# Group norm of two recurrent layers: deviations from TensorE, one variance row per head, a narrow inverse

## The reference

```python
xn = ln(x); sx = shifted(xn) - xn                  # token shift
x5 = xn + sx * (maa_stack + low_rank(xn + sx * maa_x))      # five mixes
w = exp(-exp(time_decay + tanh(x5[1] @ dw1) @ dw2))
r, k, v, g = x5[3] @ Wr.T, x5[0] @ Wk.T, x5[2] @ Wv.T, silu(x5[4] @ Wg.T)
att = scan over tokens:  out = r . (u*k*v + s);  s = k*v + w*s
m = mean(att, per head of 8); var = mean((att - m)**2, per head of 8)
att = (att - m) * rsqrt(var + 1e-5) * gn_w + gn_b    # group norm
x = x + (att * g) @ Wo.T
x = x + sigmoid(xr @ Wfr.T) * (relu(xk @ Wfk.T)**2 @ Wfv.T)  # second half
```

## Time and profile before

| what | us |
| --- | --- |
| median of three executions | 3260.69 |
| the three executions | 3263.27, 3260.69, 3254.81 |
| span of the profiled execution, first to last instruction | 3262.3 |
| the one listed execution that is no shorter than this span | 3263.27 |
| PE busy in the span | 2860.0 (88%) |
| DVE busy | 2025.3 (62%) |
| ACT busy | 1415.0 (43%) |
| POOL busy | 657.0 (20%) |

### The profile page before, as it was taken

How to read it: one execution, slowest core, us unless ns; L and a number is a source line. 1 busy time by engine, 2 the same in 40 slices (tenths; PEclk the granted TensorE clock), 3 DMA queues, 4 the chain that set the end, 5 groups by cost and what they waited for, 6 DMA issues and landing times. The chain is left out here.

```text
span 3262.3 us, 63509 instructions
## 1 busy us (share of the span) xinstructions
PE 2860.0 (88%) x18753; PEld 1510.2 (46%) x18753; DVE 2025.3 (62%) x4196; ACT 1415.0 (43%) x3023; POOL 657.0 (20%) x482
## 2 busy tenths in 40 slices
PE   6899999999999999999868888799999997888885
PEld 3344444444444444444334444466666654544443
DVE  4667776776767677677457787344444441168775
ACT  2255555555555555555612221254444443222221
POOL 4221122122112212212023333000000001033331
PEclk8799999999999999999978999799999998899997
DMA  7332433343343333334010000111110100100000
GB/s 211 107 108 75 121 108 94 103 120 102 83 122 108 86 111 111 92 101 102 16 63 1 1 1 1 54 28 34 27 34 27 34 15 29 60 1 6 6 1 12
DMA packets 117234, 205.16 MB, mean 63 GB/s; under 512 B 39765, under 2 KB 84546, under 8 KB 116546
## 3 DMA queue, kind: packets, MB, share of 16 engines
q1 hardware_dynamic: 115010, 198.32, 21.1%
q10 hardware_dynamic: 1920, 2.75, 0.4%
HBM read 156.09 MB, written 44.59 MB: 62 GB/s over the span
## 5 line engine op out<-in xcount | busy, mean ns | idle before, releaser
L596 DVE CUSTOM_DVE_ANT_0 masked<-ps_a,mask 112x750 f32<-112x750 f32 x1024 | 941.8, 936 | 383.4 <-PE ps_a L483 360.0
L556 ACT ACTIVATE probs<-ps_a 128x448 f32<-128x448 f32 (+1 forms) x1536 | 743.2, 542 | 552.7 <-PE ps_a L449 545.4
L483 PE MATMUL ps_a<-ks,q_row 96*112 96x375 bf16 x2048 | 528.3, 341 | 54.1 <-DVE part_max L596 34.9
L449 PE MATMUL ps_a<-q_sc,ks 99*128 99x448 bf16 (+1 forms) x1536 | 451.0, 359 | 52.6 <-ACT probs L556 30.9
L469 PE MATMUL ps_a<-probs,vp 128*32 128x224 f32 x6144 | 381.7, 367 | 1.2 <-ACT probs L556 0.9
L483 PEld LDWEIGHTS ps_a<-ks,q_row 96*112 96x112 bf16 x2048 | 219.9, 132 | 325.4 <-issue 266.6
L2037 DVE CUSTOM_DVE_ANT_0 f_masked<-ps_c,f_mp 112x432 f32<-112x432 f32 x256 | 145.5, 605 | 221.2 <-PE ps_c L1889 218.7
L449 PEld LDWEIGHTS ps_a<-q_sc,ks 99*128 99x128 bf16 (+1 forms) x1536 | 132.3, 100 | 287.1 <-issue 238.4
L236 POOL CAST k_piece<-kv_t 64x1500 bf16<-64x1500 f32 x32 | 45.6, 1426 | 1044.1 <-ACT kv_t L228 1044.1
L469 PEld LDWEIGHTS ps_a<-probs,vp 128*32 128x32 f32 x6144 | 164.6, 111 | 160.3 <-ACT probs L556 60.2
L215 PE MATMUL ps_a<-ctx_t,wkv 128*128 128x375 f32 x512 | 197.3, 511 | 18.6 <-DMA ctx_t<-in_ctx_t 8.5
(11 more groups left out here) (283 smaller groups left out, 3977.6 us busy)
## 6 DMA issues: line engine op xcount, KB each, us to landing
ctx_t<-in_ctx_t SPq DMA_DIRECT2D x32, 1500.0 KB, 8.9
ks<-k_scr SPq DMA_DIRECT2D x64, 562.5 KB, 5.2
mask<-in_mask SPq DMA_DIRECT2D x64, 328.1 KB, 5.5
k_scr<-k_piece SPq DMA_DIRECT2D x64, 281.2 KB, 6.6
k_scr<-k_piece SPq DMA_DIRECT2D x64, 187.5 KB, 6.8
f_context<-in_ctx_t SPq DMA_DIRECT2D x32, 375.0 KB, 3.1
k_scr<-k_piece SPq DMA_DIRECT2D x64, 93.8 KB, 7.1
q_row<-q_scr SPq DMA_DIRECT2D x64, 84.0 KB, 4.4
```

The costliest lines, as they stand in the source:

```text
L449: mm = pe.matmul(out, ks[par][:, j, at], q_sc[par][:, j], start=True, stop=not with_mask)
L483: mm = pe.matmul(ps[0:2 * L, bank + i, 0:SC], q_row[which][:, j, h, gp * 2 * L:(gp + 1) * 2 * L], ks[which][0:SROWS, j, at], start=True, s ...
L556: act.activation(probs[t % 2][0:n, i], ps[0:n, k % SCORE_BANKS, 0:PW] .rearrange("p (h n) -> p h n", h=2), ACT.Exp).then_inc(probs_done, 1)
L596: dve.tensor_tensor_reduce(out=masked[:, u % 2], in0=two_banks(bank, 2 * L), in1=in_two(mask[which][:, c * SU:(c + 1) * SU]), scale=1.0, s ...
```

## The change

The deviations are made by TensorE: `head_dev` is the identity minus the averaging matrix, so one product of it with `yo` gives `yo` minus the mean, and it goes into the bank of `Y_BANKS` that held the sum (`dev`, no longer one of the six dealt banks). ACT squares straight from PSUM. The variance is kept once per head: `head_var` has 32 columns (16 heads of each half), and eight products of 112 tokens each put four token quarters beside each other on the partitions, so one 128x112 tile holds all. Square root and reciprocal then work on 128x112. `head_of` spreads the inverse back to the channels in eight products of 112 tokens (`inv`, two of the dealt banks). ACT copies the deviations out of PSUM, scaled by half of `gn_w` (`gn_half`, made once per layer); DVE multiplies them with `inv` inside PSUM and makes `og` in one more operation. The group norm now stands whole between the second and the third pair of mixes on DVE.

```diff
 PRODUCTS = {...
-            "vb": 16, "bonus": 2, "y": 2, "mean": 2, "var": 2, "att": 2, ...}
+            "vb": 16, "bonus": 2, "y": 2, "dev": 2, "var": 1, "inv": 2, "att": 2, ...}
-TOGETHER = (("lora", 1, 2), ("var", 0, 2), ("mix", 1, 4), ("dec1", 1, 1), ...
+TOGETHER = (("lora", 1, 2), ("var", 0, 1), ("mix", 1, 4), ("inv", 0, 2), ("dec1", 1, 1), ...
...
-        for n, unit in enumerate(order):
+        turns = [unit for unit in order if unit[0] != "dev"]
+        for n, unit in enumerate(turns):
             bank[unit] = n % 6
-            before[unit] = order[n - 6] if n >= 6 else None
+            before[unit] = turns[n - 6] if n >= 6 else None
...
+                        elif name == "dev":
                             pe.wait_ge(used["y"], 2 * c + i + 1)
+                            pe.matmul(ps[:, Y_BANKS[i], 0:N], head_dev[:], yo[:, i], start=True, stop=True)\
+                              .then_inc(made["dev"], 1)
+                        elif name == "var":
                             room(unit)
+                            for k in range(KC):
+                                pe.wait_ge(s["sq"], 2 * c + k + 1)
+                                for q in range(GQ):
+                                    mm = pe.matmul(ps[32 * q:32 * q + 32, bank[unit], 0:GN], head_var[:, k],
+                                                   sq[:, k, q * GN:(q + 1) * GN], start=(k == 0),
+                                                   stop=(k == KC - 1), skip_group_check=True)
+                            mm.then_inc(made["var"], 1)
+                        elif name == "inv":
+                            pe.wait_ge(s["grs"], c + 1)
                             room(unit)
+                            for q in range(GQ):
+                                mm = pe.matmul(ps[:, bank[unit], q * GN:(q + 1) * GN], head_of[:, q, i], grs[:],
+                                               start=True, stop=True)
+                            mm.then_inc(made["inv"], 1)
...
+                        read("var", c, 0, gsd[:], ACT.Sqrt, ps[:, bank["var", 0, c], 0:GN], bias=eps[:, 0:1])\
+                            .then_inc(used["var"], 1)
                         for k in range(KC):
-                            read("var", c, k, gsd[:, k], ACT.Sqrt, bias=eps[:, 0:1]).then_inc(used["var"], 1)
+                            if c == 0:
+                                act.wait_ge(s["halved"], 1)
+                            act.activation(dev[:, k], ps[:, Y_BANKS[k], 0:N], ACT.Identity, scale=gn_half[:, k, 0:1])\
+                               .then_inc(used["dev"], 1)
...
+                def group_norm(c):
                     for k in range(KC):
+                        inv = ps[:, bank["inv", k, c], 0:N]
+                        dve.wait_ge(made["inv"], 2 * c + k + 1)
+                        dve.wait_ge(used["dev"], 2 * c + k + 1)
+                        dve.tensor_tensor(inv, dev[:, k], inv, ALU.mult).then_inc(s["scaled"], 1)
+                    for k in range(KC):
+                        inv = ps[:, bank["inv", k, c], 0:N]
+                        dve.wait_ge(s["scaled"], 2 * c + k + 1)
+                        dve.scalar_tensor_tensor(og[:, k, 0:N], inv, gn_half[:, k, 1:2], gt[:, k], ALU.add, ALU.mult)\
+                           .then_inc(used["inv"], 1)
```

More of the change, by code:

```diff
@@ L723 @@
 SUM_LAG = 4
+GQ, GN = 4, N // 4
 PRODUCTS = {"xt": 2, "lora": 2, "mix": 10, "dec1": 1, "dec2": 2, "key": 2, "val": 2, "rec": 2, "gate": 2,
-            "vb": 16, "bonus": 2, "y": 2, "mean": 2, "var": 2, "att": 2, "xt2": 2, "fk": 2, "fr": 2, "fv": 2}
+            "vb": 16, "bonus": 2, "y": 2, "dev": 2, "var": 1, "inv": 2, "att": 2, "xt2": 2, "fk": 2, "fr": 2, "fv": 2}
 TAIL = {1: "fk", 4: "fr", 7: "fv"}
-TOGETHER = (("lora", 1, 2), ("var", 0, 2), ("mix", 1, 4), ("dec1", 1, 1), ("mix", 1, 2), ("dec2", 1, 2), ("key", 1, 2),
+TOGETHER = (("lora", 1, 2), ("var", 0, 1), ("mix", 1, 4), ("inv", 0, 2), ("dec1", 1, 1), ("mix", 1, 2), ("dec2", 1, 2), ("key", 1, 2),
             ("mix", 1, 2), ("att", 0, 2), ("val", 1, 2), ("mix", 1, 2), ("rec", 1, 2), ("xt2", 0, 2), ("gate", 1, 2),
@@ L750, in product_order @@
             out.append(("bonus", 1, c))
-            out += [("mean", k, c) for k in range(KC)]
+            out += [("dev", k, c) for k in range(KC)]
         elif ahead:
@@ L780, in rwkv @@
         head_sum = sb("head_sum", [P, P])
-        head_mean = sb("head_mean", [P, P])
+        head_dev = sb("head_dev", [P, P])
+        head_var = sb("head_var", [P, KC, 32])
+        head_of = sb("head_of", [P, GQ, KC, P])
+        gn_half = sb("gn_half", [P, KC, 2])
         st = sb("st", [P, 2, KC, B])
@@ L787, in rwkv @@
                  (wo, tag + "wo"), (fk, tag + "fk"), (fr, tag + "fr"), (fv, tag + "fv"), (vsel, "vsel"),
-                 (osel, "osel"), (head_sum, "head_sum"), (head_mean, "head_mean"), (s0, "s0")]
+                 (osel, "osel"), (head_sum, "head_sum"), (head_dev, "head_dev"), (head_var, "head_var"), (head_of, "head_of"),
+                 (s0, "s0")]
         if after_layer0:
@@ L832, in rwkv @@
         names = ("first_loaded mix_loaded loaded stored preset stat0 stat1 stat2 aggr0 aggr1 aggr2 sd0 sd1 sd2 r0 r1 r2 z0 z1 z2 ln0a ln0b ln0c xhat1 xhat2 "
-                 "sxa sxb xx part mixed state rs ruk sq grs og xk2 xr2 "
-                 "sx2a sx2b kk x2 dec_w g_th summed").split()
+                 "sxa sxb xx part mixed state rs ruk sq grs xk2 xr2 "
+                 "sx2a sx2b kk x2 dec_w g_th summed halved scaled").split()
         s = {n: sem(n) for n in names}
@@ L1004, in _ @@
                 act.wait_ge(s["preset"], 6 + KC)
+                at = VEC.index("gn_w")
+                act.activation(gn_half[:], vec[:, :, at:at + 2], ACT.Identity, scale=0.5).then_inc(s["halved"], 1)
                 def deviation(c, n, which):
@@ L1063, in _ @@
                         for k in range(KC):
-                            act.wait_ge(used["mean"], 2 * c + k + 1)
-                            act.activation(sq[:, k], dev[:, k], ACT.Square).then_inc(s["sq"], 1)
+                            read("dev", c, k, sq[:, k], ACT.Square, ps[:, Y_BANKS[k], 0:N]).then_inc(s["sq"], 1)
                     if more:
@@ L2481, in layout @@
     d["head_sum"] = blocks
-    d["head_mean"] = blocks / np.float32(HS)
+    d["head_dev"] = np.eye(P, dtype=np.float32) - blocks / np.float32(HS)
+    head_var = np.zeros((16, HS, KC, KC, 16), np.float32)
+    head_of = np.zeros((GQ, KC, 16, GQ, KC, 16, HS), np.float32)
+    for h in range(16):
+        for k in range(KC):
+            head_var[h, :, k, k, h] = 1.0 / HS
+            for q in range(GQ):
+                head_of[q, k, h, q, k, h] = 1.0
+    d["head_var"] = head_var.reshape(P, KC, 32)
+    d["head_of"] = head_of.reshape(P, GQ, KC, P)
     d["st"] = c[:, 0:2].reshape(B, 2, KC, P).transpose(3, 1, 2, 0)
```

43 lines of the change are left out of this document (9 added, 34 removed).

## The result

| | before | after |
| --- | --- | --- |
| median, us | 3261.98 (four executions) | 3217.82 (four executions) |
| lowest to highest | 3254.81 to 3264.92 | 3210.86 to 3237.08 |
| profiled execution: its time, its span | 3263.27, 3262.3 | 3210.86, 3208.8 |

A forecast was written before the change was run, and what follows sets the result against it. DVE was taken to set the end of a turn through `og`, with TensorE waiting ahead of `att`. 6 x 3.45 + 2 x 5.4 = 31.5 us gave 3229 us, own range 3221 to 3240, wide range 3217 to 3247.

The forecast's parts named there:

- wide range: Whole kernel: 3217 to 3247 us, taking in the kept clock as well and leaving out 0.21 of the chance.
- six full turns: Three turns per recurrent layer: `att` starts 3.45 us earlier in each, everything behind it moves as a block.
- two last turns, up to `att`: Last turn of each layer, all of it on the path: `att` starts 5.4 us earlier.
- `att` and `fk` of the last turns, by the clock: Last turns: sum stays with 5.4 us per turn, without the 2.8 us per layer that `att` might gain.
- `gn_half` and the leads: Layer start: `gn_half` is one small operation in ACT's idle time; the added loads lie in 26.8 us of cover.
- cover ahead of the second product of `dec2`: Full turn: `og` done at 1759.2, product due at 1760.8, so 1.6 us of cover and no wait.
- the stretch ahead of the mixes: Full turn, `lora` and variance: mixes wait for `th` and start at 1751.9 instead of 1752.61.
- one gap of about 3 us: Full turn, TensorE ahead of `att`: DVE delays it through `og`; TensorE could go on about 3 us earlier.
- kept clock: Last turns: TensorE's clock stays up over short idle stretches, `att` gains another 2.8 us per layer, 3223.6 us; chance 0.25.
- Narrow products as dear as wide ones: `inv` on TensorE: 0.379 us a record, 6.1 us in all; together 2 us slower, 3262.8, no change; chance 0.08.
- The next scan takes it back: Scans start earlier only to wait more; six turns bring nothing, 10.8 us are left, 3249.9; chance 0.08.
- Operations inside PSUM are dear: DVE's operations writing PSUM: at 2.94 us each the kernel is 30.6 us slower, 3291; chance 0.05.

The follow-up runs named there:

- experiment 8: Experiment 6 with its scan-end fill products widened to 448 columns, two of them ahead of the last sum: 3200.97 us, ratio 0.9836.
- experiment 3: Kernel before with only the deviations made by `head_dev` on TensorE and read from PSUM, DVE's subtractions gone: 3254.29 us, ratio 0.9979.
- experiment 5: Kernel after with unused fill products ahead of `inv`, `att`, `xt2` and `fk` in each layer's last turn: 3210.01 us, ratio 0.9859.
- experiment 7: Kernel before with twelve unused fill products ahead of `att` in the last turn of each layer: 3254.73 us, ratio 0.9993.
- experiment 6: Experiment 5 plus one 224-column fill product ahead of each of the last four sums of every scan: 3205.43 us, ratio 0.9845.
- experiment 1: Kernel after with two added 128x448 reciprocals on DVE, behind the third pair of parts in each full turn: 3223.76 us, ratio 0.9887.
- experiment 4: Kernel after with the group norm's end in three operations per half again, deviations copied unscaled: 3223.67 us, ratio 0.9889.
- experiment 2: Kernel after with each narrow product of `inv` issued twice: 3239.57 us, ratio 0.9931.
- experiment 9: Kernel before with only the small `gn_half` operation on ACT at each layer's start, result unused: 3255.36 us, one execution.

## Why the prediction was right, step by step

The mechanism of the prediction held, and it gave 31.5 us where the change brings 37.3. From the median it started from that is 3223.4 us, inside the forecast's own range of 3221 to 3240. The measured median, 3217.82, lies below that and 0.8 us inside the wide range; that it did not fall out of it is luck, for the executions after lie 26 us apart. By its terms:

| term | forecast, us | measured, us |
| --- | --- | --- |
| six full turns | 20.7 | 19.7 |
| two last turns, up to `att` | 10.8 | 11.4 |
| `att` and `fk` of the last turns, by the clock | 0 | 4.0 + 0.6 |
| `gn_half` and the leads | 0 | 1.4 |
| scans | 0 | 0.2 |

*Full turns.* The forecast had `att` 14.35 us behind the first mixes; it was 14.31 in all six. The prices: variance 0.59 us (0.7 forecast), square root 0.35 (0.35), reciprocal 0.84 (0.86), `inv` to `dec1` 1.87 (1.9), the multiplication inside PSUM 0.63 (0.62). `og` took 0.68 per half, not 0.62. The cover ahead of the second product of `dec2` was 1.8 us in the first turn (`og` done at 1745.58, the product due at 1746.60 + 0.75), 1.6 forecast. `dec2` does not wait, and the loads cost nothing that the leads show. What fell short is the stretch ahead of the mixes: 0.5 us gained on the average instead of 0.7. In the first turn of b, for which the forecast was made, it gained nothing: `lora` took 3.90 us there and 3.19 before. The length of this stretch, 5.94 to 7.29 us, depends on when the clock rises in `lora`; at the full clock (experiment 8) it is 5.34 in all six turns.

*Where the 2.79 us come from.* The prediction has one gap of about 3 us that DVE makes, ahead of `att`, as the weight loads waited there. In the trace before, TensorE itself has three gaps between the first mixes and `att` of the first turn of b: 1.43 us ahead of `dec1`, which waits for POOL, 2.13 ahead of `att`, and this one, in the order of all engines, ahead of the third pair of mixes, which waits for DVE's `part`:

```profile
1765.84 1.74 PE L933 MATMUL ps_b<-b_th,b_w 128*128 128x448 f32 x4 [0.85 <-DVE b_part L1183]
```

Together they are 4.41 us. After the change none of them is left, and `inv` takes 1.87 us in their place, which makes 2.54 of the 2.79. In experiment 3 the second and third gap are 0.55 and 1.82, so DVE held TensorE up in two places. The prediction's sum took in all three, since it laid TensorE's products one behind the other.

*The last turns.* To `att` they gained 5.7 us each, 5.4 forecast. The step that was mis-sized is the clock, a term that the sum put at nothing: the prediction left `att` at 6.50 us and gave the kept clock a chance of 0.25 as a rival, with 2.8 us per layer. The rival came true in d (2.77) and half in b (6.62 to 5.41 us, 1.21). The 0.6 us of `fk` come from the same cause. Experiments 5 and 7 show that it is the clock: filled, `att` takes 3.72 us in both kernels, whatever else the turn does. The Trainium skill (TensorE: Matmul & The Clock Gate, Part 1: The HAM clock gate) says that activity releases the throttled state; experiments 5, 7 and 8 agree. But in experiment 6 the granted clock stayed at 0.50 in layer d over 3.00 us of work. Why b lost it in the middle of `att` and d did not, with the same order of work and the same idle stretches, these runs do not settle; in experiment 1 both kept it (3.73 and 3.72 us), in experiment 4 neither (5.41 in both). So the 4.0 us of `att` are what this trace had, and not a fixed part of the change. That the whole comes to about the 37.1 us of this rival is chance, for 1.4 us of it are the leads.

*The rivals.* "Narrow products as dear as wide ones" falls with 0.112 us a record (experiment 2). "The next scan takes it back" falls with scans of 394.4 and 394.2 us and with `att` to `kv` at 19.60 us in all turns. "Operations inside PSUM are dear" falls with 0.63 and 0.68 us.

*What the prediction did not see.* `gn_half` was priced at nothing as "one small operation in ACT's idle time". It gained 1.4 us, by releasing a table load (experiment 9). And the deviations alone bring 0.61 us per turn behind the mixes, because DVE and POOL no longer hold each other up (experiment 3); the prediction had that inside DVE's freed time. A slip without effect: by its own chances the prediction has 0.83 for faster and 0.12 for no change, not 0.84 and 0.11.

## What to carry to other kernels

Count what an off-path engine is waited for, not what it is busy: DVE lost 81 us here, and the turn gained until TensorE had no gap left, 2.8 us, after which 5.75 us more on DVE cost nothing. Where one engine stands alone on the path, as in the last turns, every step counts, and there the clock of TensorE is a term of its own: price such a stretch at both levels, and try products whose result is thrown away in its gaps, which took 17.6 us off two last turns and six full ones in the traces here (ratio 0.9836 beside 0.9884). A small operation that can run early on ACT may take a table load with it, as `gn_half` did.

## What was not expected of the hardware

- The clock falls late: in experiment 2 it was 1.00 for more than 1 us of work behind the idle stretch and then 0.50 for the stretch from 3192 to 3194, while TensorE was busy all of it.
- A multiply-add in SBUF takes 0.51 us alone and 1.79 to 2.15 beside POOL's `mixed`. The same holds for a tiny one: of the kernel after, first turn of b, DVE and POOL in order of time, and then the same operation in the last turn of d:

```profile
1761.94 2.07 POOL L1361 TENSOR_TENSOR b_mixed<-b_part,b_xn 128x896 f32<-128x896 f32 x1 [6.27 <-DVE b_part L1205]
1762.07 1.97 DVE L1137 SCALAR_TENSOR_TENSOR b_shift<-b_mv,b_rstd 128x4 f32<-128x4 f32 x1
...
3177.45 0.16 DVE L1137 SCALAR_TENSOR_TENSOR d_shift<-d_mv,d_rstd 128x4 f32<-128x4 f32 x1
```

Four elements per partition take 1.97 us beside POOL and 0.16 without. This one lies in the 19.60 us from `att` to `kv` that nothing here has shortened; moving it was not tried.
